# Moving GpSimd's scatter of routed rows ahead of the second norm in an adaLN, linear-attention and mixture-of-experts kernel

## What is computed

```python
h = _layernorm(x) * (1 + ca) + sa
x = x + ga * attention(h)          # phi_q, phi_k by exp; cumulative sums of phi_k v and phi_k
h = _layernorm(x) * (1 + cb) + sb  # the second norm
# experts: two largest of softmax(h @ wg); position of each token in its expert by a
# cumulative count; tokens over the capacity (1024 a expert) are dropped
disp = zeros((E, cap, D)).at[e_flat, p_flat].add(x_rep * kmask)   # the scatter
y = gelu(disp @ w1 + b1) @ w2 + b2
x = x + gb * sum_of_two(y[e_flat, p_flat] * weight)
```

## Time and profile before

| what | value |
|---|---|
| time, median of 3 runs | 730.0 us (729.62 to 730.08) |
| the profiled execution: span from first to last instruction | 811.6 us |
| what lies around the span | shown by no view |
| granted TensorE clock, mean | 0.952 of full speed |
| PE, DVE, ACT, POOL busy | 92%, 66%, 47%, 41% of the span |
| indirect DMAs of the scatter | 64, 1.05 us each on POOL |

### The profile page before, as it was taken

The page is one execution under the profiler, slowest core; times in us unless marked ns, Lnnn a source line. Parts: engine busy times, 40 slices in busy tenths (PEclk is TensorE's granted clock), DMA queues, the critical chain, the costliest instruction groups (busy, mean ns, idle before and its releaser), DMA issues. The chain is left out here.

```text
span 811.6 us, 27349 instructions
## 1 busy us (share of the span) xinstructions
PE 744.8 (92%) x11452; PEld 637.3 (79%) x11452; DVE 538.3 (66%) x1685; ACT 382.7 (47%) x740; POOL 335.7 (41%) x625
## 2 busy tenths in 40 slices
PE   8999899999999999999999999999999889999957
PEld 8788778777777777887777888878777678989943
DVE  6678667667666676766666777677666635556425
ACT  5656444444444455544444555455444124344310
POOL 3114443444444444444444444444433622555650
PEclk9999999999999999999999999999999999999979
DMA  9871000000000000000000000000000044435218
GB/s 270 340 282 55 13 8 7 12 9 13 8 10 9 9 9 9 9 9 9 9 9 9 9 9 9 9 9 10 9 8 10 16 120 138 152 118 154 79 50 302
DMA packets 32705, 47.25 MB, mean 58 GB/s; under 512 B 4132, under 2 KB 20168, under 8 KB 32584
## 3 DMA queue, kind: packets, MB, share of 16 engines
q1 hardware_dynamic: 23296, 32.62, 12.2%
q0 software_dynamic: 4096, 8.42, 3.2%
q10 hardware_dynamic: 5192, 4.47, 1.7%
HBM read 22.21 MB, written 23.36 MB: 56 GB/s over the span
## 5 line engine op out<-in xcount | busy, mean ns | idle before, releaser
L648 ACT COPY v_sb<-bank 128x512 f32<-128x512 f32 x64 | 37.6, 587 | 181.2 <-PE bank L279 179.4
L348 PE MATMUL bank<-v_sb,scores 64*64 64x65 f32 x2048 | 69.5, 224 | 30.0 <-issue 28.8
L1297 POOL DMA_INDIRECT y_rows<-y_sb,row_id x64 | 63.5, 993 | 68.3 <-DVE y_sb L1442 51.2
L1038 POOL TENSOR_TENSOR h_lo<-h_full,h_hi 128x192 fp32r<-128x192 f32 x32 | 19.0, 594 | 168.3 <-ACT h_hi L641 168.3
L348 PEld LDWEIGHTS bank<-v_sb,scores 64*64 64x64 f32 x2048 | 51.2, 133 | 42.3 <-issue 42.2
L768 DVE SCALAR_TENSOR_TENSOR expo_q<-norm_q,bank 128x512 f32<-128x512 f32 x64 | 43.9, 688 | 50.4 <-PE bank L279 49.4
L1108 POOL DMA_INDIRECT dispatched<-h_cur,slot x64 | 67.2, 1050 | 17.8 <-issue 16.1
L1376 ACT ACTIVATE hidden<-bank,b_col 128x512 f32<-128x512 f32 x64 | 41.4, 687 | 59.9 <-PE bank L1348 38.2
L632 ACT ACTIVATE phi_k<-expo_k 128x1024 f32<-128x1024 f32 x32 | 33.9, 1058 | 74.1 <-DVE expo_k L768 71.5
L893 DVE SCALAR_TENSOR_TENSOR mid<-bank,state 128x260 f32<-128x260 f32 x56 | 24.0, 428 | 62.9 <-remote 48.6
L527 PEld LDWEIGHTS bank<-woT,attT 128*128 128x128 f32 x512 | 61.9, 191 | 3.1 <-ACT attT L738 0.6
(11 more groups left out here) (243 smaller groups left out, 2101.8 us busy)
## 6 DMA issues: line engine op xcount, KB each, us to landing
dispatched<-blank SPq DMA_DIRECT2D x16, 524.0 KB, 3.0
region<-dispatched SPq DMA_DIRECT2D x30, 262.0 KB
y_rows<-blank SPq DMA_DIRECT2D x8, 512.0 KB, 4.0
w_nat<-in_L_ffn_w_dram SPq DMA_DIRECT2D x8, 256.0 KB
y_got<-y_rows SPq DMA_DIRECT2D x8, 256.0 KB, 6.9
y_got<-y_rows ACTq DMA_DIRECT2D x8, 256.0 KB, 7.8
out_dram<-x_sb SPq DMA_DIRECT2D x8, 256.0 KB, 3.8
w_sb<-in_L_ffn_w_dram ACTq DMA_DIRECT2D x6, 256.0 KB
```

Of the source, the lines that this page charges most:

```text
L348: mm = pe.matmul(out(i, z, side), scores[keys, (2 * g + z) * 4 + i, :], v_sb[par][keys, 8 * z + 4 * g + i, :], start=(j == 0 and side == 0 ...
L1297: pool.indirect_dma_start(out=y_rows[:, :], out_offset=bass.IndirectOffsetOnAxis(ap=row_id[par][:, t:t + 1].bitcast(U32), axis=0), in_=y_s ...
```

## The change

In each step from c = 2 to c = 31 POOL calls `scatter()` right behind the sum of residual and attention result, ahead of `rstd` of the second norm, where before it stood at the end of the step. In step 33, which has no second norm to make, it stays where it was; step 32 has its own call and is not touched. Waits, instructions and buffers are the same.

```diff
@@ step() of POOL, in "if live(c, -1):"
                                 pool.tensor_tensor(x2_now[:], xs, upd[1][:], ALU.add).then_inc(sem("x2_ready"), 1)
+                                if last:
+                                    scatter()
                                 rstd(pool, "ln2", var2, rs2, c)
                                 pool.wait_ge(sem("x2_ready"), c)
                                 pool.tensor_copy(xs, x2_now[:])
...
                                 pool.tensor_tensor(h2_cur[nxt][:, 0:D], xm2[:], sb_b[:, own], ALU.add).then_inc(sem("h2_ready"), 1)
-                            if last:
+                            if c == NCH + 1:
                                 scatter()
-                            if isinstance(c, int) and c == 1:
+                            if c == 1:
```

## The result

The changed kernel takes 733.49 us (733.35 to 735.34, 4 runs), the kernel before 729.81 us on the same chip (729.18 to 730.08, 4 runs): ratio 1.0056 [1.0041, 1.0072], 0.4 to 0.7% slower. The forecast was 733.4 us. How it came to so near a number is another matter, since two of its terms were off and cancelled.

What follows compares the result with a forecast made beforehand. PE was taken as the bound, busy 92% of the span, its hold-up beside POOL's indirect DMAs belonging to the recording. 2.55 + 0.2 + 0.7 = 3.45 us on 730.0 gave 733.4 us, range 731.5 to 735.

Steps and rivals of the forecast that it cites:

- The main term: Step 31, PE at L507: no projection covers the later `h2_cur`, so the delay counts in full, +2.55 us.
- Rival (c): The wait in step 31 doesn't show; time 730 us within 1.4; chance 0.10.
- Steady steps: Steps 2 to 30: the later `h2_cur` stays hidden from PE at L507 by 0.62 us of slack; cost 0.
- rival (b): `h2_cur` comes too late for PE in every step, 0.6 us x 28 = 17 us, 750 us; chance 0.12.
- The clock term: After PE's longer idle in step 31 the clock may fall to 1.2 GHz; +0.7 us, bounds 0 and +1.46.
- Step 32: PE waits up to 0.75 us for `h2_cur`, mostly covered by its wait for `hot`; +0.2 us.
- The hold-up: PE's matmuls at L348 beside POOL's indirect DMAs: 93.5 us in the recorded execution, taken as 0 in a plain run.
- rival (a): The hold-up is partly there without a recording; up to 8.3 us saved, 11.9 if it vanishes; chance 0.21.
- the term "0": The hold-up of PE at L348 in the plain run, taken as 0 with 11.9 us as upper bound.
- the forecast span of 741 us: Recorded execution of the changed kernel: 718.1 + 28 x 0.7 + 3.45 = 741 us, some 70 us shorter.
- the 11.9 us around the span: Plain run: 730.0 - 718.1 us, left for all around the span and any hold-up without a recording.
- 0.7 us a step: Hold-up of PE's dense work still expected in the recorded execution at the scatter's new place, 0.7 us in each step.

Runs made afterwards that it cites:

- kernel 2: Changed kernel with the early scatter in steps 2 to 29 only, steps 30 and 31 as before the change; 729.24 us, ratio 0.9989 to the kernel before.
- kernel 3: Kernel before with the early scatter in steps 30 and 31 only; 734.81 us, ratio 1.0065 to the kernel before.
- kernel 4: Kernel before with the early scatter in step 30 only; 735.59 us, ratio 1.007 to the kernel before.
- kernel 6: As kernel 2, with one more unread POOL sum behind each moved scatter; 729.46 us, ratio 0.9977 to the kernel before.
- kernel 7: As kernel 2, with two more unread POOL sums behind each moved scatter; 731.67 us, ratio 1.001 to the kernel before.
- kernel 5: As kernel 4, with 22 useless PE transposes ahead of step 31's wait for `h2_cur`; 733.02 us, ratio 1.0025 to the kernel before.
- kernel 9: Kernel before with 128 useless instructions (64-row matmuls) added in PE's opening, shifting its stream; 727.73 us, ratio 0.9962 to the kernel before.
- kernel 11: As kernel 2, with the same 128 instructions (64-row matmuls) in PE's opening as kernel 9; 725.87 us, ratio 0.9929 to the kernel before.
- experiment 8: As kernel 2, with 32 useless matmuls (128 instructions) at PE's beginning, to test its lone gaps; 734.51 us, ratio 1.0047 to the kernel before.

## Why the prediction was right, and where it was not

**The main term held.** Step 31 has no projection to hide the later `h2_cur`: predicted +2.55 us, measured 2.81 instead of 0.48, +2.33. The place is shown by kernels 2 to 4. The chain that leads there was right nearly to the hundredth: begin of the DMA 0.85 us after the slots (0.86), `h2_cur` 7.55 to 7.58 us after `upd` (7.55). Rival (c) fell with it: the wait shows.

**Steady steps.** PE's slack of 0.62 us was right, shown by kernels 6 and 7, and rival (b) fell: the first DMA took 1.12 us, 0.93 of them beside DVE's 1.21 us reduction, no more than elsewhere. What I had held against that rival was weak: the 1.19 us scatter of the earlier trace rows ran beside no long copies, only for 0.32 us beside one DVE instruction with two operands (`wq_lo`, 653.20 to 653.89).
The Trainium skill ("SBUF — State Buffer", Who interferes with whom) has a `tensor_reduce` never contend with GpSimd on trn2, so the blocking by two-port operations that the prediction cites does not bear on this reduction. The trace agrees: 1.12 us beside it, 1.13 away from it.

**The clock term was mis-sized.** Taken +0.7 us (0 to 1.46), measured about 2.7 by kernels 4 and 5. I had priced a fall by the mean difference of slow and full windows in the steady loop, over stretches which half-speed work fills only in part. Behind the wait of step 31, 6.83 us ran at 0.52, with PE busy for 6.47 of them.

**Step 32.** Taken +0.2 us; the wait came (0.58 us), was made good at `hot` (0.55 us less), and cost nothing, as kernel 4 beside kernel 3 shows.

**The hold-up was put in the wrong place.** I took the 93.5 us as belonging to the recording and 0 for the plain run. Recording is not what makes it: a later record of the same kernel spans 729.3 us and its run took 2.1 us more. The plain kernel does have a hold-up, 4.5 us in the loop, so rival (a) was true in its mechanism, just below the 4.9 us from which it would have decided. It did not decide because 3.9 us came back as lone gaps of PE, a thing in none of my cases. So the term "0" was right as a sum (-0.6 us) and wrong as a reason. For the same reason the forecast span of 741 us and the 11.9 us around the span were wrong; 2.0 us lie around it. At the new place no hold-up is seen, where I had reckoned 0.7 us a step.
The Trainium skill ("Runtime: NRT & Kernel Launch", The launch sequence) has 9 to 15 us around a kernel; the measured time here holds 2.0 us beside the span. Whether the rest lies outside of what is measured, no run shows.

**The sum.** Predicted 2.55 + 0.2 + 0.7 = 3.45 us. Measured 2.33 + 0 + 2.66 = 4.99 of the 5.09 us in the tail, and -0.56 in the loop: 4.5 us in all; the medians say 3.7. The pair of profiled executions has +2.2 us in its spans, because the part behind the tail, which the change does not touch, was 1.8 us shorter in the changed kernel's record (149.91 against 151.74) and the part ahead of the loop 0.5. Such differences between single executions are as large as the error of the sum, so 733.4 against 733.49 is partly luck.

**What stays open.** Why the first record of the kernel before lost 2.4 us a step beside the indirect DMAs (10.71 against 8.31 at full clock), where the repeated one loses 0.23 (16.50 against 16.27), was not found. That PE's lone gaps are waits for packets of instructions rests on the times of the two, not on a row that names the releaser. How much the early scatter is worth without them is not shown by medians: kernels 9 and 11 overlap.

## What to carry to other kernels

Moving work ahead on one engine is free only in the steps in which the waiter has other work; look at the first and the last steps one by one, since a pipeline that drains has lost its cover, and leave the move out there (kernel 2). A wait of a few us on PE costs more than itself when dense work follows it at the lower clock, so price the work behind the wait, not a mean over the loop. Where the profiled span and the plain time differ by much more than the few us of other records, record the kernel again before building a sum on it.

## What the runs showed of the hardware

- PE's small matmuls are held up while POOL issues an indirect DMA: 0.87 us instead of 0.65 for those of L348 in ordinary executions, without an idle that a table of waits would list, and by 2.4 us a step in one execution.
- Where a dense stream of instructions stands matters: 128 instructions more in the opening made the loop 6.6 to 9.3 us shorter, whichever of the three kernels they were put in (486.48 to 479.92, 485.92 to 476.66, 485.83 to 476.98). The page of the changed kernel has the loads of instructions as a queue of their own (packets, MB, share):

```profile
q8 instruction: 91, 1.49, 0.9%
```

  1.49 MB in 91 packets is 16.4 KB each; the shifted kernels have 92. No row names such a packet as what a gap waits for, but every gap ends 1.2 to 1.6 us after one (experiment 8). The gaps also keep a measure: in the unshifted records they stand multiples of some 125 matmuls apart (3472, 3596 and 4473 matmuls into PE's work, say), and in the shifted ones half of that off. 125 matmuls with their loads of weights are 250 instructions, of which the added 128 are half.
  The Trainium skill ("Runtime: NRT & Kernel Launch", Instruction fetch mechanics) has instructions refilled in blocks of 16 KiB, at a cost that is mostly hidden. The size agrees with the packets; by that reading of the gaps the cost is not hidden here, 6.6 us of a loop in the repeated kernel before and 10.3 in the changed one.
- As many added instructions, 128, cost 13.66 us as 128-row matmuls at the opening's start and 2.04 us as 64-row ones some 4 us later. Whether the rows or the place makes the difference, no run shows.
